# Four cross-attention layers on one core: every step placed anew, and unused matmuls ahead of some waits in the first two turns

## The reference, cut to what matters

```python
# layer 0: 16 heads of 8, key j allowed for query i where j < i, the first query's row is zero
q, k, v = x @ Wq + bq, ctx @ Wk + bk, ctx @ Wv + bv
a = softmax(where(allowed, q k^T / sqrt(8), -1e30));  a[:, :, 0, :] = 0
x = layer_norm(x + (a v) @ Wo + bo);  x = layer_norm(x + relu(x @ W1 + b1) @ W2 + b2)
# layer 1: 16 heads of 8, no mask
x = x + attention(x, ctx);  x = x + gelu(x @ W1 + b1) @ W2 + b2
# layer 2: one vision vector a sequence, vis = mean(ctx) @ Wv^T + bv
agree = sum((x @ Wt^T + bt) * vis);  r = softmax(2 * agree over the tokens)
fused = x + sigmoid(gate(x, r * vis)) * r * vis;  x = layer_norm(fused)
# layer 3: 16 heads of 64, on the rms-normed x
x = x + softmax(q k^T) v @ wo
```

## Time and profile before

| | us |
|---|---|
| runs shown | 1546.59, 1545.48, 1546.05 (median 1546.05) |
| profiled execution | 1548.49, of which the span is 1546.8 |
| PE busy | 1421.6 (92% of the span) |
| DVE, ACT, POOL busy | 1079.5, 975.0, 489.8 |
| PE's clock, mean of the execution | 0.982 of full |

### The profile page before, as it was taken

How to read it: one execution, slowest core, us unless ns; L and a number is a source line. 1 busy time by engine, 2 the same in 40 slices (tenths; PEclk the granted TensorE clock), 3 DMA queues, 4 the chain that set the end, 5 groups by cost and what they waited for, 6 DMA issues and landing times.

```text
span 1546.8 us, 53472 instructions
## 1 busy us (share of the span) xinstructions
PE 1421.6 (92%) x22629; PEld 1046.0 (68%) x22629; DVE 1079.5 (70%) x2644; ACT 975.0 (63%) x1877; POOL 489.8 (32%) x522
## 2 busy tenths in 40 slices
PE   5679999999999999999999999899999999999877
PEld 3446776767677676867667686676767677676655
DVE  4467768686786867778686877768687786866643
ACT  3246667666676766667676666667666676756554
POOL 2132423314252331525233151423315142331402
PEclk9789999999999999999999999999999999999999
DMA  4000000000000000000000000000000000000000
GB/s 140 14 1 15 3 9 16 9 16 10 15 3 9 16 10 15 10 15 3 9 16 9 16 10 15 3 8 16 10 15 3 22 3 9 2 10 1 3 8 9
DMA packets 27816, 20.31 MB, mean 13 GB/s; under 512 B 1088, under 2 KB 27200, under 8 KB 27328
## 3 DMA queue, kind: packets, MB, share of 16 engines
q1 hardware_dynamic: 27584, 16.90, 3.7%
HBM read 12.70 MB, written 4.19 MB: 11 GB/s over the span
## 4 chain that ended last, share of the span: by engine, by line
PE 83%; DVE 6%; issue 4%; POOL 3%; ACT 3%; DMA 0%; SPq 0%; ACTq 0%; DVEq 0%
PE bank L487 68%; PE bank L496 15%; DVE z L1075 2%; POOL rstd L902 2%; ACT prob L854 1%; DVE stats L1061 1%; DVE negmax L1017 1%; POOL var_eps L899 1%; POOL prob L895 1%; ACT prob L782 1%; POOL w_low L886 0%; DVE mv L1066 0%; ACT Q L867 0%; DMA vec<-in_vectors 0%; DVE sums L1022 0%
## 5 line engine op out<-in xcount | busy, mean ns | idle before, releaser
L895 POOL TENSOR_TENSOR prob<-prob,rinv 128x512 f32<-128x512 f32 x256 | 263.6, 1042 | 361.5 <-DVE rinv L1024 359.2
L496 PE MATMUL bank<-cst,prob 128*128 128x128 f32 x1536 | 217.8, 279 | 14.9 <-POOL prob L915 6.0
L496 PEld LDWEIGHTS bank<-cst,prob 128*128 128x128 f32 x1536 | 180.2, 143 | 54.9 <-issue 27.5
L789 ACT ACTIVATE probT<-bank 128x512 f32<-128x512 f32 x256 | 144.8, 600 | 92.2 <-PE bank L496 90.6
L782 ACT ACTIVATE prob<-bank 128x512 f32<-128x512 f32 x256 | 146.9, 604 | 82.0 <-PE bank L487 81.9
L1022 DVE TENSOR_REDUCE sums<-prob 128x8 f32<-128x512 f32 x256 | 171.0, 668 | 38.9 <-ACT prob L782 37.7
L1017 DVE TENSOR_REDUCE negmax<-bank 128x8 bf16<-128x512 f32 x256 | 162.9, 674 | 46.3 <-PE bank L487 45.7
L915 POOL TENSOR_TENSOR prob<-prob,rinv 128x512 f32<-128x512 f32 x128 | 132.0, 1042 | 198.5 <-DVE rinv L1168 198.1
L899 POOL TENSOR_TENSOR var_eps<-mv,ln_eps 128x4 f32<-128x4 f32 x48 | 14.9, 310 | 455.1 <-DVE mv L1066 455.1
L487 PE MATMUL bank<-negmax,ident_b 128*128 128x512 bf16 x384 | 134.9, 391 | 11.6 <-DVE negmax L1017 8.7
L854 ACT ACTIVATE prob<-bank,rms_rows 128x256 f32<-128x256 f32 x256 | 103.9, 482 | 64.6 <-PE bank L487 62.3
(11 more groups left out here) (155 smaller groups left out, 2953.3 us busy)
## 6 DMA issues: line engine op xcount, KB each, us to landing
x_in<-in_x SPq DMA_DIRECT2D x16, 256.0 KB, 3.0
c_in<-in_ctx SPq DMA_DIRECT2D x16, 256.0 KB, 3.3
out<-y SPq DMA_DIRECT2D x16, 256.0 KB, 2.3
Q<-in_split_weights SPq DMA_DIRECT2D x1, 1536.0 KB, 8.9
wt<-in_weights SPq DMA_DIRECT2D x1, 1024.0 KB, 10.7
wt<-in_weights SPq DMA_DIRECT2D x1, 640.0 KB, 5.7
wt<-in_weights SPq DMA_DIRECT2D x4, 128.0 KB, 10.3
cst<-in_constants SPq DMA_DIRECT2D x1, 229.0 KB, 2.7
```

The costliest lines, as they stand in the source:

```text
L496: last = nc.tensor.transpose(o[:, k * P:(k + 1) * P], src(k), ident)
L789: nc.scalar.activation(probT[:, t].rearrange("p s q -> p (s q)"), bank("PT", l, u, t)[:, :], ACT.Identity).then_inc(probT_ready.sem, 1)
L895: nc.gpsimd.tensor_tensor(pr, pr, ri, ALU.mult).then_inc(norm_ready.sem, 1)
```

## The change

Three things, and nothing else (SP's program, the steps and what each computes are the same):

1. In place of one `PLAN` with `START` and `AHEAD` there are five: for turn 0, turn 1, turns 2 to 13, turn 14 and turn 15, each for all four engines, at a uniform distance `TURN` of 89.7521. Every list is new. The bank of each tile comes from one table for each of the five plans.
2. In the plan of the middle turns the tiled steps stand further apart on PE: of their direct neighbours four pairs a turn (S.0.1 O.0.0, S3.0 S3.1, O3.1 S.1.1, O3.3 O.1.1) become three (S.0.1 O.0.0, S3.2 O3.0, O.1.0 S.1.1). Over the whole program 64 such pairs become 46.
3. At 13 places of turns 0 and 1 the step first does 2 to 6 matmuls of 128x512 bf16 with `ident_b` into its own bank, 36 in all, whose result is overwritten; they wait for the bank and for `constants_done`, and only then does the step wait for its operands.

```diff
-START = [0, 89.64, 179.32, 268.97, ...]
-AHEAD = {("K3", 0): -0.08, ...}
+TURN = 89.7521
+PLANS = {2: PLAN, 0: {...}, 1: {...}, 3: {...}, 4: {...}}
+def plan_of(group):
+    return {0: 0, 1: 1, G - 2: 3, G - 1: 4}.get(group, 2)
+
+WARM = {("xT", (), 0): 6, ("q", (0,), 0): 2, ("k", (0,), 0): 4, ("O", (0, 0), 0): 2, ("O", (0, 1), 0): 2, ("o", (0,), 0): 4,
+        ("lnT", (0,), 0): 2, ("k3", (0,), 0): 3, ("h", (0, 0), 0): 2, ("S", (0, 0), 1): 2, ("q", (1,), 0): 2,
+        ("S", (1, 0), 0): 2, ("PT", (1, 1, 0), 0): 3}
...
-    placed = [(START[g] + at - AHEAD.get((kind, g), 0.0), kind, index, g) for g in range(G) for kind, index, at in plan]
+    placed = [(TURN * g + at, kind, index, g) for g in range(G)
+              for kind, index, at in map(parse, PLANS[plan_of(g)][engine].split())]
...
+                if (kind, index, g) in WARM:
+
+                    if kind in ("S", "O"):
+                        for t in range(QUAD if kind == "S" else 2):
+                            for empty in freed(g, kind, *index, t):
+                                pe.wait_ge(*empty)
+                    pe.wait_ge(constants_done, 2)
+                    own = bank(g, kind, *index, 0) if kind in ("S", "O") else bank(g, kind, *index)
+                    for _ in range(WARM[kind, index, g]):
+                        mm(own[:, :], ident_b[:, :], ident_b[:, :].unsqueeze(1).broadcast_to([P, CH, P]))
```

More of the change, by code:

```diff
@@ L53 @@
     "PE": """
[L54 to L68, removed]
@@ L89 @@
-    "DVE": """
[L90 to L102, removed]
@@ new lines @@
+        PT.0.0.0@389.5784 PT.0.0.3@390.5672 S.0.1@393.3857 O.0.0@393.4608 shift.0.1.2@393.7216 shift.0.1.3@396.6965
+        shift.0.1.0@397.3054 shift.0.1.1@398.1073 PT.0.1.2@399.3188 PT.0.1.0@400.8561 PT.0.1.3@401.9676 PT.0.1.1@404.1541
+        O.0.1@405.0739 o.0@407.5423 vis@407.5777 lnT.0@410.9972 lnF.0@416.1891 gv@416.4535 h.0.0@418.4547 h.0.2@418.5238
+        h.0.1@421.0854 h.0.3@421.2492 f.0.0@422.2398 f.0.1@422.9658 f.0.2@423.196 f.0.3@424.1805 lnT.1@427.0152 lnF.1@432.662
+        q.1@435.8339 k.1@436.9117 S.1.0@441.676 shift.1.0.0@444.8576 shift.1.0.2@445.0007 shift.1.0.1@447.321
@@ new lines @@
+        v3.4@498.2541 v3.6@499.2964 v3.3@501.0457 k3.0@501.627 k3.6@501.6807 k3.3@502.2278 v3.0@502.4578 v3.7@503.4343
+        lnT.2@503.9044 lnF.2@511.7578 q3.2@516.0274 q3.6@516.9318 q3.3@519.1754 q3.0@519.6628 q3.1@519.7888 q3.4@520.7886
+        q3.7@523.7917 q3.5@524.6579 rows@524.9672 S3.0@525.7332 shift3.0.0@526.8302 shift3.0.1@528.8122 S3.1@528.9016
+        shift3.1.1@532.5578 PT3.0.0@533.0614 shift3.1.0@533.2775 PT3.0.1@533.38 S3.2@535.615 O3.0@535.9968 PT3.1.0@538.0246
+        shift3.2.0@538.1307 PT3.1.1@538.4787 shift3.2.1@540.2104 S3.3@541.1685 out3.0@541.2979 shift3.3.0@542.6991
@@ L539, in step @@
                     pe.wait_ge(*c_low_ready(g))
[L540 removed]
+                    o = bank(g, "v", u)
                     for i in range(2):
@@ L621, in step @@
                     pe.wait_ge(*z_ready(g, n))
-                    transpose4(bank("lnF", n), lambda k: z[n // 2][:, k, :]).then_inc(lnF_filled.sem, 1)
+                    transpose4(bank(g, "lnF", n), lambda k: z[n // 2][:, k, :]).then_inc(lnF_filled.sem, 1)
                 elif kind == "h":
@@ L726, in step @@
                     for p in range(PAIRS):
-                        last = mm(bank("out3")[:, k * P:(k + 1) * P],
+                        last = mm(bank(g, "out3")[:, k * P:(k + 1) * P],
                                   Q3[:, p, 2 * k:2 * k + 2, :].rearrange("p b q -> p (b q)"),
@@ L795, in step @@
                         act.wait_ge(*lnT_filled(g - 1, 2))
-                    nc.scalar.activation((x1T[0], x2T)[n][:, :], bank("lnF", n)[:, :], ACT.Identity,
+                    nc.scalar.activation((x1T[0], x2T)[n][:, :], bank(g, "lnF", n)[:, :], ACT.Identity,
                                          bias=v(f"ln{n + 1}_b"), scale=v(f"ln{n + 1}_g")).then_inc(ln_out.sem, 1)
@@ L1060, in step @@
                     for k in range(CH):
-                        last = nc.vector.bn_stats(stats[l][:, k, :], bank("lnT", n)[:, k * P:(k + 1) * P])
+                        last = nc.vector.bn_stats(stats[l][:, k, :], bank(g, "lnT", n)[:, k * P:(k + 1) * P])
                     last.then_inc(stats_ready.sem, 1)
@@ L1074, in step @@
                     for k in range(CH):
-                        last = nc.vector.tensor_scalar(z[l][:, k, :], bank("lnT", n)[:, k * P:(k + 1) * P], mv[l][:, k, 0:1],
+                        last = nc.vector.tensor_scalar(z[l][:, k, :], bank(g, "lnT", n)[:, k * P:(k + 1) * P], mv[l][:, k, 0:1],
                                                        rstd[l][:, k:k + 1], ALU.subtract, ALU.mult)
```

451 lines of the change are left out of this document (359 added, 92 removed), and 15 rows, old and new, of the table BANK.

## The result

The changed kernel takes 1534.58 us (median of five, 1532.87 to 1539.2) against 1546.05: ratio 0.9934, 95% interval 0.9915 to 0.9954. It is faster, as forecast, inside the range, but by 11.5 us and not by 20. Its profiled execution took 1534.58 us too (span 1533.0), 13.9 less than the one of before.

The account below looks back on a forecast made before the run. PE's own steps plus its waits bound the kernel. From the profiled 1548.49 us, -8.4 (middle) -3.5 (start) -6 -2 (last turns) = -19.9 gives 1528.6; as a median 1526, range 1507 to 1549.

Parts of the forecast that it names:

- last sign: Closing failure test: the forecast fails if the start keeps its +9 us or the middle turns' period isn't lower at all.
- Middle turns: Turns 2 to 13, priced over turns 1 to 14: fewer stalls and bank waits, -0.6 us a turn, -8.4 us together.
- new tight places: Middle turns: O.1.0 follows its last PT with too little other PE work, +0.4 us a turn, ends 0 and +0.8.
- rival B: Middle turns: stalls only move with block borders and other waits come back elsewhere, 0 a turn; 1537 us, chance 0.20.
- The start: Turns 0 and 1: later first steps against filled waits and higher clock, sum -3.5 us, ends +12 and -12.
- Step (a): Start: six unused matmuls wait for constants_done; xT +6.8 us, q.0 about 5.4 later, w_low ends at about 32.
- Step (b): Start: k3.2 ahead of S.0.0 waits for w_low; S.0.0 +14.5 us, about +10 behind last PT, +9 at O.0.1.
- Rival A: Slower: the start's delay is never made good; start +11, middle 0, end -3, 1554 us, chance 0.12.
- (c) to (e): Start: steps moved into waits -3.5 and +2 us, clock -4 and -2, PE filled between 68 and 108 us -5.
- Step (d): Start: PE at half clock in 45.8 to 62.8 and 93.6 to 100.4 us; fuller waits win -4 and -2 us.
- Rival E: Unused matmuls stand where PE doesn't wait or don't lift the clock; 1533 us, chance 0.11.
- The end: Last turns: steps moved into waits before ag, lnF.2, q3 and q3's clock, -6 us; "issue" of last two turns, -2.

## Why the prediction was right, and where it was not
**The sum.** 1526 forecast, 1534.58 measured: -19.9 against -11.5 by the medians and -13.9 by the profiled executions. Of the four terms one was right, one wrong as a whole, one of the wrong size for a reason not counted, one near. In the traces they came as +2.1, -1.3, -5.8 and -8.8, for -8.4, -3.5, -6 and -2. By its own last sign the forecast fails in the middle turns, whose period isn't lower at all; that the total still lies in the range is partly luck, since the turns 14 and 15 gave back what the middle didn't bring.

**Middle turns, forecast -8.4, measured about 0.** The two main steps came as worked out, even larger: "issue" 0.65 a turn less (forecast 0.5), exp's bank wait 0.84 less (0.5). What failed is the step "sum -0.6 a turn": each removed wait was taken off the period. In its place PE waits for POOL (+0.41 a turn, 0.32 without the stall at 986.6), probT (+0.35) and z (+0.12), is busy 0.46 a turn longer (why isn't known; 0.2 was forecast for the switches), and has gaps too short for the list of waits: the listed ones fell by about 9 us, all idle time by 4.0. I had put the new tight places at 0.4, which was right for O.1.0 alone; I had no term for POOL. The page gave a hint: the chain had DVE, POOL and ACT at 12% before, and has them at 19% after. One slip that changed nothing: the term's ends, -1.6 and +0.6, aren't the sums of its parts' ends, -2.75 and +0.8. That a turn of before could be replaced by the new one without any change (91.0 and 90.9 us, six and eight traces) is rival B's result, by another mechanism than its first one: fewer stalls did happen. Which loop over the four engines holds the 90.9 wasn't tried.

**The rule on fetches.** The Trainium skill, "Runtime: NRT & Kernel Launch", Instruction fetch mechanics, gives 256 instructions to a block, and 128 instructions more moved the stalls by one turn; that agrees. That the fetch is hidden by the issue floor, as the Trainium skill says in the same place, doesn't hold in tiled steps: stalls of up to 1.85 us at the block borders were seen. (The prediction's 17 ns are those of a matmul; with its weight load, an instruction of its own, it is half: 128 instructions in 1.16 us.)

**The start, forecast -3.5, measured -1.3 in the trace and nothing by the median (0.9998).** Step (a): xT +6.8, measured +6.4; but q.0 ended 2.6 us later, not 5.4: it began 3.7 later (13.66 and 17.35), and its two matmuls took 1.02 us behind the unused ones, not 2.08; w_low was done at 29, not 32, and the first norm began at 36.7, not 38 to 39. Step (b): S.0.0 +14.5, measured +12.1; +10 behind its last PT, measured +8; +9 at O.0.1, measured +8.9. That k3.2 held up the chain is shown: with k3.2 moved away S3.0 of turn 0 ends 7 us earlier, and without the first dummies another 4. Rival A named it and its price; what it had wrong is that it is not made good, since (c) to (e) brought back 10 us by O.1.1 (-1.1). Step (d) was right on the clock (from 0.50 to 0.80 and 1.00 in the two short stretches of the earlier trace rows) and wrong on its cause and worth: the denser order raised it, the dummies hardly (0.97 over 25 to 160 us without them, 0.93 with).

**Rival E**, that the dummies don't do what they say, holds in its result: 24 of 36 are worth nothing that can be seen (1525.66 against 1524.7), and the first twelve cost 4 us in the trace and 7 by the median once k3.2 is out of the way; the difference may be the blocks. I had priced them at 2.6 us and credited the clock.

**The end, forecast -6 and -2.** From o.1 of turn 15 on: 69.0 to 70.0 us in five traces with the order of before, 63.2 to 64.9 in nine with the new one, -5.7: the steps moved into the waits before ag, lnF.2 and q3, and q3's clock, were sized right. Where the -2 for "issue" in turns 14 and 15 was put, the whole stretch from S3.0 of turn 13 to o.1 of turn 15 is 8.8 us shorter in this pair of traces. There the step that failed was to take stalls as a rate. They are places: before had a bad one in turn 14, and the clock fell behind it. A shift of the blocks by padding removed it, with no new order at all. From S3.0 of turn 13 to o.1 of turn 15 the order of before took 134.8, 132.8, 128.6, 125.7 and 125.1 us in five traces, the new one 123.9 to 126.4 in nine: the nine are as good as before's best. So a part of the measured 11.5 us is likely not the new order's as such, but where its blocks happen to fall; how much stays open. The padded kernels' 3 to 5 us don't size it, since they were mostly made in the start.

## What to carry to other kernels
Count a removed wait as gained only after asking which engine is late next; a chain in which the other engines hold 12% gives back little of what one engine saves. In a program without loops, time a change against padded versions of both kernels: 64 and 32 matmuls that compute nothing made the kernel before 3 to 5 us faster here, against 11.5 for the whole change, and in the traces single stretches differed by up to 10. To find such stalls, count the engine's instructions in the trace and look at the place of each unexplained gap in its 256. Put no step that waits for a late operand ahead of the head of a dependent chain, and no filler ahead of an input's first use: both together cost 10 us by the medians, 11.4 at S3.0 of turn 0 in the traces.
